# Taking the logarithm of the sums of squares straight out of PSUM, with the floor of the norm turned into a ceiling on its reciprocal

## The chip, the cores and the metric

The kernel runs on one core of one Trainium2 chip. The metric is the device time of one execution in microseconds (us), from the first to the last instruction of the core with what lies around it. A core has five engines that run side by side, each taking its own instructions in order: TensorE (PE, matrix multiplies; its weight loads are shown as PEld), VectorE (DVE), ScalarE (ACT), GpSimd (POOL) and SyncE (SP), which here only starts DMAs. They wait for each other through semaphores.

## The reference

The input is 8 sequences of 512 tokens with 128 features. A first block adds a causal attention with 16 heads. The second block, which the change concerns, is a stack of six layers. Each layer shifts half of the features by one token, projects to queries, keys and values of 16 heads of 64, divides each query and each key by its length, applies a rotary table, attends within windows of 32 tokens and projects back; then it runs a gated feed-forward part behind a layer normalisation:

```
def l2norm(t):
    return t / jnp.maximum(jnp.linalg.norm(t, axis=-1, keepdims=True), 1e-12)
...
q = l2norm(q) * qs
k = l2norm(k) * ksc
```

What is asked is the exact division by the norm, with a floor of 1e-12 on the norm.

## The kernel before

Stage 1 (the first block) is not touched. Stage 2 holds the residual of all tokens in SBUF and goes, in each of six layers, through 8 sequences, and each sequence in 8 steps: four groups of four heads (a quad) by two halves of 256 tokens. A step's work is a pipeline over several steps: the projection of a quad-half is made in step n, its sum of squares, logarithm and exponential in step n+1, the scaled queries and keys in n+2, scores and softmax in n+3, the weighted values in n+4 and the output projection in n+5 (LAG_MIX to LAG_WO are 1 to 5). The order of work on each engine is written out by hand in one function `step` per engine. After the 8 sequences a layer drains for six steps (s == NSEQ) and runs its feed-forward part; the next layer fills the pipeline anew.

The normalisation takes this way. ScalarE squares the projections (line 935, tile sq, 128x1024). GpSimd adds the two halves of each head (line 824). TensorE sums over the features of a head with a matrix of ones into one PSUM bank, ss_bank (line 1198). VectorE copies that bank to inv_norm in SBUF with a floor of 1e-24 (line 1064, called the guard below, semaphore guard_done). ScalarE takes the logarithm of it in place (line 950, Ln) and then exp(-0.5 x) (line 953, Exp). One step later VectorE multiplies the rotated queries and keys by it in one instruction (line 783, write_qk, tile qk).

The order within a step, around the change:

- TensorE: scores (lines 1167, 1177), transposes of the softmax (1157), sums of squares (1198), values (1209 to 1211), projections (1222 to 1224), weighted values (1246), output projection (1259). In step 5 of all sequences but the first it then makes the mean of the layer normalisation of the sequence before (ffn_mean, line 1130), and in step 6 the variance (ffn_var, line 1134). Both write ss_bank, which the sums of squares use too, so both wait until that bank has been read in this step: `pe.wait_ge(S["guard_done"], n)`.
- ScalarE: copy of the transposed softmax (891), four exponentials (901), copy of the values (924), in step 6 a square for the layer normalisation (868), four exponentials, Square (935), the copy of y out of PSUM (943), Ln (950), Exp (953).
- VectorE: row minima (1020), a copy of the transposed softmax (1047), write_qk (783), guard (1064), two reciprocals (1027), and the two products with the rotary tables (1082, 1087). In step 5 a residual add (1033) stands ahead, in step 6 the centring (991).
- GpSimd: the add of the squares (824), two adds for the rotation (802), in step 3 the rest of the tokens of the next sequence (815, tokens_rest), then two multiplications of the softmax by the inverse sums (811), each waiting for its reciprocal.

Of the kernel before, what the change touches and what calls it, by code (L numbers as in the profile page):

```python
# [21 lines left out]
ACT = mybir.ActivationFunctionType  # L22
ALU = mybir.AluOpType
# [563 lines left out]
LN_SCALE = 2.0 ** 16  # L587
NORM_FLOOR = 1e-24


def build_stage2(nc, d, res_sb, u_sb, out, depth):

    with ExitStack() as st:
        def sb(name, shape, dt=F32):
            return st.enter_context(nc.sbuf_tensor(name, shape, dt))

        def sem(name):
# [27 lines left out]
        eps = sb("s2_eps", [P, 1])  # L625
        ln_shift = sb("s2_ln_shift", [P, 1])

        xs_raw = sb("s2_xs_raw", [P, WIN + SEQ])
# [32 lines left out]
        names = ("const_in consts cast zeroed attn_w ffn_w tables w_high w_rest xs_in xs_high xs_rest proj_done sq_done sqadd_done prod_done "  # L661
                 "add_done ss_done guard_done log_done inv_done norm_done score_done max_done exp_done "
                 "rden_done probs_done tr_done pt_first pt_second v_mm v_done v_moved0 v_moved1 v_moved2 v_moved3 pv_done y_done wo_done attn_res "
# [18 lines left out]
        def live(s, p, lag, first):  # L682

            if first:
                return p >= lag
            return p < lag if s == NSEQ else True
# [4 lines left out]
        def place(p, lag):  # L691

            m = (p - lag) % STEPS
            return m // 2, m % 2, m % 2
# [83 lines left out]
        def write_qk(p):  # L778

            quad, toks, par = place(p, LAG_NORM)  # L780
            at = WIN + toks * TOKS
            by = inv_norm[:, par, :, :].unsqueeze(2).to_broadcast([P, 2, 2, TOKS])
            return nc.vector.tensor_tensor(qk[:, quad % 2, :, :, at:at + TOKS], rotated[:, par, :, :, :], by, ALU.mult)  # L783

        @block.gpsimd
        def _(pool):
# [6 lines left out]
            pool.memset(ln_shift[:, :], 0.5 * float(np.log(LN_SCALE))).then_inc(S["consts"], 1)  # L793
            pool.wait_ge(S["consts"], 4)

# [67 lines left out]
        def _(act):  # L863
            act.wait_ge(S["consts"], 4)

# [11 lines left out]
            def step(l, s, p, first):  # L877
# [52 lines left out]
                if full:  # L930

                    act.wait_ge(S["proj_done"], n + 1)
                    if not (first and p == 0):
                        act.wait_ge(S["ss_done"], n)
                    nc.scalar.activation(sq[:, :, :, :], proj_ps[:, :, :, :], ACT.Square)\  # L935
                      .then_inc(S["sq_done"], 1)
                if live(s, p, LAG_VALUE, first):
                    m = n - LAG_VALUE
                    act.wait_ge(S["pv_done"], m + 1)

                    if not (first and p < LAG_VALUE + 2):
                        act.wait_ge(S["wo_done"], m - 1)
                    nc.scalar.activation(y[:, place(p, LAG_VALUE)[2], :, :],
                                         vy_bank[:, :].rearrange("p (a t) -> p a t", a=2), ACT.Copy)\
                      .then_inc(S["y_done"], 1)
                if live(s, p, LAG_MIX, first):

                    m, par = n - LAG_MIX, place(p, LAG_MIX)[2]
                    act.wait_ge(S["guard_done"], m + 1)
                    nc.scalar.activation(inv_norm[:, par, :, :], inv_norm[:, par, :, :], ACT.Ln, scale=LN_SCALE)\  # L950
                      .then_inc(S["log_done"], 1)
                    act.wait_ge(S["log_done"], m + 1)
                    nc.scalar.activation(inv_norm[:, par, :, :], inv_norm[:, par, :, :], ACT.Exp, scale=-0.5,
                                         bias=ln_shift[:, 0:1]).then_inc(S["inv_done"], 1)
# [25 lines left out]
        def _(dve):  # L980
# [4 lines left out]
              .then_inc(S["cast"], 1)  # L985
            dve.wait_ge(S["consts"], 4)
            dve.wait_ge(S["cast"], 2)
# [23 lines left out]
            def step(l, s, p, first):  # L1011
# [38 lines left out]
                if norm:  # L1050
# [6 lines left out]
                    write_qk(p).then_inc(S["norm_done"], 1)  # L1057
                if live(s, p, LAG_MIX, first):
                    m, par = n - LAG_MIX, place(p, LAG_MIX)[2]
                    dve.wait_ge(S["ss_done"], m + 1)  # L1060

                    if not (first and p < LAG_MIX + 2):
                        dve.wait_ge(S["norm_done"], m - 1)
                    nc.vector.tensor_scalar(inv_norm[:, par, :, :].rearrange("p a t -> p (a t)"), ss_bank[:, :],
                                            NORM_FLOOR, None, ALU.max).then_inc(S["guard_done"], 1)
                if score:
# [56 lines left out]
        def _(pe):  # L1123
            pe.wait_ge(S["const_in"], 48)
            pe.wait_ge(S["consts"], 4)
            pe.wait_ge(S["cast"], 2)
# [17 lines left out]
            def step(l, s, p, first):  # L1144
# [41 lines left out]
                if live(s, p, LAG_MIX, first):  # L1186
# [3 lines left out]
                    if not (first and p == LAG_MIX):  # L1190
                        pe.wait_ge(S["guard_done"], m)

# [83 lines left out]
                if full and not first and p in (LN_STEP, LN_STEP + 1):  # L1276

                    pe.wait_ge(S["guard_done"], n)
                    (ffn_mean if p == LN_STEP else ffn_var)(l * NSEQ + s - 1)
# [142 lines left out]
```

## Time and profile before

| | us |
|---|---|
| runs shown: median (lowest to highest) | 4187.51 (4180.85 to 4187.87) |
| the profiled execution's own time | 4182.92 |
| its span, first to last instruction | 4181.1 |
| PE busy | 3900.5 (93%) |
| DVE busy | 3305.5 (79%) |
| ACT busy | 3091.6 (74%) |
| POOL busy | 2581.2 (62%) |

Stage 1 fills about the first 700 us; the six layers are alike after that, some 577 us each. The mean granted TensorE clock is 0.986 of full speed. "Busy" counts the time in which an engine has an instruction under way, and that includes time in which the instruction itself is held up inside the engine. Matmuls overlap, so their recorded durations are longer than what each adds to the chain.

### The profile page before, as it was taken

The numbers are of one execution on the slowest core, as the hardware profiler recorded it, in microseconds if no ns is written. First come the engines' busy times: TensorE is split into PE (matmuls) and PEld (weight loads), VectorE is DVE, ScalarE is ACT, GpSimd is POOL, SyncE is SP. The second block draws the span as 40 slices with busy tenths as digits, with TensorE's granted clock in tenths as the row PEclk, the third lists the DMA queues.
The fourth block names the chain that finished last, engine by engine and source line by source line (L and its number), as shares of the span: only waits on it lengthen the run. The fifth ranks groups of instructions, "written<-read, shape, count | busy, mean of one in ns | idle before, by whom it ended". The sixth has DMA issues, their size and how long they took to land.

```text
span 4181.1 us, 190344 instructions
## 1 busy us (share of the span) xinstructions
PE 3900.5 (93%) x78816; PEld 3039.7 (73%) x78816; DVE 3305.5 (79%) x5294; ACT 3091.6 (74%) x10376; POOL 2581.2 (62%) x2583
## 2 busy tenths in 40 slices
PE   6888885999998999989999989999899999899998
PEld 3555554888866888848888668888488887588884
DVE  6778874988866888938888668989489886698894
ACT  5877785888865888838888658888488886588883
POOL 4667765766645676627666456766377664566660
PEclk9999998999999999999999999999999999999999
DMA  1000001111111111111111111111111111111110
GB/s 35 2 2 2 2 2 53 47 45 45 46 56 38 45 47 45 44 50 44 49 44 46 58 36 47 44 49 42 53 44 47 47 44 61 35 45 46 47 43 26
DMA packets 100195, 167.40 MB, mean 40 GB/s; under 512 B 26224, under 2 KB 33648, under 8 KB 99056
## 3 DMA queue, kind: packets, MB, share of 16 engines
q1 hardware_dynamic: 99312, 154.89, 12.6%
q8 instruction: 644, 10.55, 1.1%
q14 instruction: 239, 1.96, 0.2%
HBM read 26.13 MB, written 2.10 MB: 7 GB/s over the span
## 4 chain that ended last, share of the span: by engine, by line
PE 69%; issue 9%; POOL 3%; DVE 1%; ACT 0%; DMA 0%; SPq 0%; POOLq 0%; DVEq 0%; ACTq 0%
PE s_bank L1177 13%; PE s_bank L1246 10%; PE s_bank L1259 9%; PE s_bank L1198 8%; PE s_bank L1157 5%; PE s_proj L1222 4%; PE s_proj L1223 4%; PE s_proj L1224 4%; PE s_bank L1209 2%; PE s_bank L1210 2%; PE s_bank L1211 2%; PE s_bank L1167 2%; PE s_bank L1140 1%; POOL s_rotated L802 1%; PE s_bank L1289 1%
## 5 line engine op out<-in xcount | busy, mean ns | idle before, releaser
L802 POOL TENSOR_TENSOR s_rotated<-s_rotated,s_by_sin 128x512 f32<-128x512 f32 x768 | 983.8, 1302 | 227.3 <-DVE s_by_sin L1087 225.2
L811 POOL TENSOR_TENSOR s_probs<-s_probs,s_rden 128x256 f32<-128x256 f32 x768 | 479.7, 641 | 729.8 <-DVE s_rden L1027 729.3
L901 ACT ACTIVATE s_probs<-s_bank,s_neg_max 128x64 f32<-128x64 f32 x3072 | 908.0, 310 | 5.7 <-DVE s_neg_max L1020 5.6
L783 DVE TENSOR_TENSOR s_qk<-s_rotated,s_inv_norm 128x1024 f32<-128x1024 f32 x384 | 743.8, 1937 | 11.5
L1082 DVE TENSOR_TENSOR s_rotated<-s_proj,s_cos 128x1024 f32<-128x1024 f32 x384 | 469.6, 1223 | 241.5 <-ACT s_sq L935 240.9
L901 ACT ACTIVATION_READ_ACCUMULATOR s_probs<-s_bank,s_neg_max 128x1 f32 x3072 | 636.1, 207 | 0.0
L891 ACT ACTIVATE s_probs_t<-s_bank 64x512 f32<-64x512 f32 x384 | 226.8, 591 | 524.8 <-PE s_bank L1157 524.8
L1177 PE MATMUL s_bank<-s_qk 32*32 32x64 f32 x49152 | 581.4, 223 | 26.3 <-issue 25.9
L1177 PEld LDWEIGHTS s_bank<-s_qk 32*32 32x32 f32 x49152 | 510.9, 103 | 115.4 <-issue 114.6
L213 POOL TENSOR_TENSOR s_probs<-s_probs,s_rden 128x384 f32<-128x384 f32 (+3 forms) x512 | 406.4, 802 | 206.1 <-DVE s_rden L406 202.2
L824 POOL TENSOR_TENSOR s_sq<-s_sq 128x512 f32<-128x512 f32 x384 | 490.2, 1277 | 65.5 <-ACT s_sq L935 59.8
L1087 DVE TENSOR_TENSOR s_by_sin<-s_proj,s_sin 128x1024 f32<-128x1024 f32 x384 | 466.2, 1214 | 0.0
L1246 PE MATMUL s_bank<-s_probs_t,s_v 128*64 128x64 f32 x12288 | 445.5, 226 | 21.8 <-ACT s_probs_t L891 17.1
L1246 PEld LDWEIGHTS s_bank<-s_probs_t,s_v 128*64 128x64 f32 x12288 | 393.0, 138 | 77.1 <-ACT s_probs_t L891 21.4
L1198 PE MATMUL s_bank<-s_sq,s_same_head 128*128 128x256 f32 x1536 | 403.9, 386 | 40.2 <-POOL s_sq L824 37.9
L1222 PE MATMUL s_proj<-s_xs_high,s_w_high 128*128 128x256 f32 x1536 | 437.1, 285 | 0.0
L1259 PE MATMUL s_bank<-s_y,s_wo 128*128 128x256 f32 x1536 | 436.9, 407 | 0.0
L1223 PE MATMUL s_proj<-s_xs_rest,s_w_high 128*128 128x256 f32 x1536 | 436.6, 284 | 0.0
L1224 PE MATMUL s_proj<-s_xs_high,s_w_rest 128*128 128x256 f32 x1536 | 435.2, 283 | 0.0
L935 ACT ACTIVATE s_sq<-s_proj 128x1024 f32<-128x1024 f32 x384 | 397.8, 1036 | 25.2 <-PE s_proj L1224 25.2
L1020 DVE TENSOR_REDUCE s_neg_max<-s_bank 128x4 f32<-128x256 f32 x768 | 289.0, 418 | 72.1 <-PE s_bank L1177 69.1
L295 ACT ACTIVATE s_probs<-s_bank,s_neg_max 128x384 f32<-128x384 f32 (+3 forms) x512 | 271.9, 533 | 89.3 <-DVE s_neg_max L397 85.7
(118 smaller groups left out, 8156.2 us busy)
## 6 DMA issues: line engine op xcount, KB each, us to landing
s_v<-s_v SPq DMA_DIRECT2D x384, 192.0 KB, 2.5
s_v<-s_v SPq DMA_DIRECT2D x384, 64.0 KB, 2.4
s_qk<-f_wqk SPq DMA_DIRECT2D x6, 1024.0 KB, 6.4
s_xs_raw<-u SPq DMA_DIRECT2D x48, 128.0 KB
s_xf<-u SPq DMA_DIRECT2D x48, 128.0 KB, 2.3
s_xs_raw<-u SPq DMA_DIRECT2D x48, 127.8 KB
s_xf<-u SPq DMA_DIRECT2D x48, 127.8 KB, 2.6
s_qk<-f_wv SPq DMA_DIRECT2D x6, 512.0 KB, 6.8
```

The costliest lines, as they stand in the source:

```text
L783: return nc.vector.tensor_tensor(qk[:, quad % 2, :, :, at:at + TOKS], rotated[:, par, :, :, :], by, ALU.mult)
L802: nc.gpsimd.tensor_tensor(rotated[:, par, :, half, :], rotated[:, par, :, half, :], by_sin[:, :, 1 - half, :], (ALU.subtract, ALU.add)[half])\
L811: nc.gpsimd.tensor_tensor(part, part, by, ALU.mult).then_inc(S["probs_done"], 1)
L824: nc.gpsimd.tensor_tensor(sq[:, :, 0, :], sq[:, :, 0, :], sq[:, :, 1, :], ALU.add)\
L901: last = nc.scalar.activation(probs[:, par, h, b, :], score_bank[h][:, b * KEYS:(b + 1) * KEYS], ACT.Exp, scale=-1.0, bias=neg_max[:, par, ...
L1177: last = nc.tensor.matmul(score_bank[e][to:to + WIN, w * KEYS:(w + 1) * KEYS], qk[rows, quad % 2, 0, c, WIN + at:WIN + at + WIN], qk[rows, ...
L1198: last = nc.tensor.matmul(ss_bank[:, i * TOKS:(i + 1) * TOKS], same_head[:, :], sq[:, i, 0, :], start=True, stop=True)
L1222: nc.tensor.matmul(proj_ps[:, i, c, :], w[0], xs_high[:, s % 2, at:at + TOKS], start=True, stop=False)
L1223: nc.tensor.matmul(proj_ps[:, i, c, :], w[0], xs_rest[:, s % 2, at:at + TOKS], start=False, stop=False)
L1224: last = nc.tensor.matmul(proj_ps[:, i, c, :], w[1], xs_high[:, s % 2, at:at + TOKS], start=False, stop=True)
L1246: last = nc.tensor.matmul(mixed[HD * h:HD * (h + 1), pair, t, :, e, :], v[:, cols, (half * NT + t) * 2 + e, at:at + HD], probs_t[:, e, t, ...
L1259: last = nc.tensor.matmul(wo_bank[:, half * TOKS:(half + 1) * TOKS], wo[:, 2 * quad + pair, :], y[:, par, pair, :], start=(p == LAG_WO and ...
```

## The change

VectorE's guard goes away. ScalarE's Ln now reads ss_bank in PSUM itself, with a small bias that takes the place of the floor, and moves ahead of the copy of y, right behind Square. The floor on the norm becomes a ceiling of 1e12 on its reciprocal, applied inside write_qk, which becomes two instructions of another kind (scalar_tensor_tensor, 128x512 each: minimum with a constant, then product) in place of one of 128x1024. Whatever waited for guard_done now waits for log_done: the next sums of squares on TensorE, and the mean and the variance of the layer normalisation, which share the bank. One small memset for the bias is added at the start.

```diff
@@ write_qk
-            by = inv_norm[:, par, :, :].unsqueeze(2).to_broadcast([P, 2, 2, TOKS])
-            return nc.vector.tensor_tensor(qk[:, quad % 2, :, :, at:at + TOKS], rotated[:, par, :, :, :], by, ALU.mult)
+            for i in range(2):
+                by = inv_norm[:, par, i, :].unsqueeze(1).to_broadcast([P, 2, TOKS])
+                last = nc.vector.scalar_tensor_tensor(qk[:, quad % 2, i, :, at:at + TOKS], by, NORM_CUT,
+                                                      rotated[:, par, i, :, :], ALU.min, ALU.mult)
+            return last
@@ ScalarE, step: between Square and the copy of y
+                if live(s, p, LAG_MIX, first):
+
+                    m, par = n - LAG_MIX, place(p, LAG_MIX)[2]
+                    act.wait_ge(S["ss_done"], m + 1)
+                    if not (first and p < LAG_MIX + 2):
+                        act.wait_ge(S["norm_done"], m - 1)
+                    nc.scalar.activation(inv_norm[:, par, :, :].rearrange("p a t -> p (a t)"), ss_bank[:, :], ACT.Ln,
+                                         scale=LN_SCALE, bias=log_floor[:, 0:1]).then_inc(S["log_done"], 1)
@@ ScalarE, step: behind the copy of y
-                    act.wait_ge(S["guard_done"], m + 1)
-                    nc.scalar.activation(inv_norm[:, par, :, :], inv_norm[:, par, :, :], ACT.Ln, scale=LN_SCALE)\
-                      .then_inc(S["log_done"], 1)
                     act.wait_ge(S["log_done"], m + 1)
@@ VectorE, step: behind write_qk
-                if live(s, p, LAG_MIX, first):
-                    m, par = n - LAG_MIX, place(p, LAG_MIX)[2]
-                    dve.wait_ge(S["ss_done"], m + 1)
-
-                    if not (first and p < LAG_MIX + 2):
-                        dve.wait_ge(S["norm_done"], m - 1)
-                    nc.vector.tensor_scalar(inv_norm[:, par, :, :].rearrange("p a t -> p (a t)"), ss_bank[:, :],
-                                            NORM_FLOOR, None, ALU.max).then_inc(S["guard_done"], 1)
@@ TensorE, step: ahead of the sums of squares, and ahead of the mean and the variance
-                        pe.wait_ge(S["guard_done"], m)
+                        pe.wait_ge(S["log_done"], m)
...
-                    pe.wait_ge(S["guard_done"], n)
+                    pe.wait_ge(S["log_done"], n)
                     (ffn_mean if p == LN_STEP else ffn_var)(l * NSEQ + s - 1)
```

## Rows read from the trace of the kernel before

**Rows 1.** Busy us by stretch: its length, PE, PEld, DVE, ACT, POOL, clock, DMA.

```profile
1386.50:1756.30 369.80, 365.25 (x9098) 312.82 (x9097) 329.41 (x457) 303.35 (x1080) 252.27 (x246) 1.00 0.16 46
```

**Rows 2.** Chain that ended last: start, us it adds, what; ends of steps 5 and 6.

```profile
1509.92 0.86 PE s_bank L1130 x2
...
1518.12 0.86 PE s_bank L1134 x2
```

**Rows 3.** Waits over the whole span: who for whom, us, times, longest.

```profile
POOL s_probs L811 <- DVE s_rden L1027: 729.3, 392, 6.6
ACT s_probs_t L891 <- PE s_bank L1157: 524.8, 384, 5.0
PE s_bank L1177 <- issue: 25.9, 41, 2.3
...
PE s_bank L1157 <- issue: 8.1, 12, 0.9
```

**Rows 4.** Timeline, step 5 of one sequence: start us, us, instruction, [idle before].

```profile
1507.17 0.69 DVE L1064 TENSOR_SCALAR s_inv_norm<-s_bank 128x512 f32<-128x512 f32 x1
...
1508.18 1.03 ACT L935 ACTIVATE s_sq<-s_proj 128x1024 f32<-128x1024 f32 x1
...
1509.08 0.61 ACT L943 ACTIVATE s_y<-s_bank 128x512 f32<-128x512 f32 x1
...
1509.76 1.02 PE L1130 MATMUL s_bank<-s_xf,s_mean_w 128*128 128x512 f32 x2
```

**Rows 5.** Timeline, step 6 of the same sequence.

```profile
1516.90 1.03 ACT L935 ACTIVATE s_sq<-s_proj 128x1024 f32<-128x1024 f32 x1
...
1517.80 0.61 ACT L943 ACTIVATE s_y<-s_bank 128x512 f32<-128x512 f32 x1
...
1517.95 1.02 PE L1134 MATMUL s_bank<-s_rstd,s_mean_w 128*128 128x512 f32 x2
```

**Rows 6.** Single lines: ns min/median/max, first and last start us.

```profile
L873 ACT ACTIVATE s_rstd<-s_bank,s_eps x48: 666/668/688, 819.5 to 4126.7; 128x512 f32<-128x512 f32 x48
...
L1134 PE MATMUL s_bank<-s_rstd,s_mean_w x96: 590/592/593, 817.8 to 4126.1; 128*128 128x512 f32 x96
```

**Rows 7.** Timeline in stage 1: a matmul that waits for ScalarE.

```profile
227.16 0.63 ACT L253 ACTIVATE s_sq<-s_xc 128x512 f32<-128x512 f32 x1
227.84 1.13 PE L451 MATMUL s_bank<-s_sq,s_mean_w 128*128 128x512 f32 x2 [0.47 <-ACT s_sq L253]
```

**Rows 8.** VectorE's groups: busy us, mean ns of one, idle before.

```profile
L783 DVE TENSOR_TENSOR s_qk<-s_rotated,s_inv_norm 128x1024 f32<-128x1024 f32 x384 | 743.8, 1937 | 11.5
L1082 DVE TENSOR_TENSOR s_rotated<-s_proj,s_cos 128x1024 f32<-128x1024 f32 x384 | 469.6, 1223 | 241.5 <-ACT s_sq L935 240.9
...
L1064 DVE TENSOR_SCALAR s_inv_norm<-s_bank 128x512 f32<-128x512 f32 x384 | 265.5, 691 | 14.2 <-PE s_bank L1198 2.8
...
L1092 DVE SCALAR_TENSOR_TENSOR u<-s_bank,s_vec,u 128x512 f32<-128x512 f32 x48 | 36.1, 751 | 63.0 <-PE s_bank L1289 63.0
```

**Rows 9.** Timeline of a step 3, and the sums of squares of step 4.

```profile
1366.51 2.52 POOL L802 TENSOR_TENSOR s_rotated<-s_rotated,s_by_sin 128x512 f32<-128x512 f32 x2 [0.44 <-DVE s_by_sin L1087]
...
1367.85 2.27 DVE L783 TENSOR_TENSOR s_qk<-s_rotated,s_inv_norm 128x1024 f32<-128x1024 f32 x1
...
1368.99 2.33 POOL L815 TENSOR_TENSOR s_xs_rest<-s_xs_raw,s_xs_high 128x544 fp32r<-128x544 f32 x1
...
1371.29 1.18 POOL L811 TENSOR_TENSOR s_probs<-s_probs,s_rden 128x256 f32<-128x256 f32 x2
...
1372.43 1.28 POOL L824 TENSOR_TENSOR s_sq<-s_sq 128x512 f32<-128x512 f32 x1
...
1374.01 0.73 PEld L1198 LDWEIGHTS s_bank<-s_sq,s_same_head 128*128 128x128 f32 x4
```

**Rows 10.** Timeline, step 3 while a layer's pipeline fills.

```profile
1888.63 1.87 DVE L783 TENSOR_TENSOR s_qk<-s_rotated,s_inv_norm 128x1024 f32<-128x1024 f32 x1
...
1891.52 0.38 PE L1167 MATMUL s_bank<-s_band_b,s_ident_b 128*128 128x256 bf16 x2 [1.20 <-ACT s_probs L901]
```

More of the change, by code:

```diff
@@ L587 @@
 LN_SCALE = 2.0 ** 16
-NORM_FLOOR = 1e-24
+NORM_CUT = 1e12
+LOG_FLOOR = LN_SCALE * 1e-32
 def build_stage2(nc, d, res_sb, u_sb, out, depth):
@@ L626, in build_stage2 @@
         ln_shift = sb("s2_ln_shift", [P, 1])
+        log_floor = sb("s2_log_floor", [P, 1])
         xs_raw = sb("s2_xs_raw", [P, WIN + SEQ])
@@ L661, in build_stage2 @@
         names = ("const_in consts cast zeroed attn_w ffn_w tables w_high w_rest xs_in xs_high xs_rest proj_done sq_done sqadd_done prod_done "
-                 "add_done ss_done guard_done log_done inv_done norm_done score_done max_done exp_done "
+                 "add_done ss_done log_done inv_done norm_done score_done max_done exp_done "
                  "rden_done probs_done tr_done pt_first pt_second v_mm v_done v_moved0 v_moved1 v_moved2 v_moved3 pv_done y_done wo_done attn_res "
@@ L793, in _ @@
             pool.memset(ln_shift[:, :], 0.5 * float(np.log(LN_SCALE))).then_inc(S["consts"], 1)
-            pool.wait_ge(S["consts"], 4)
+            pool.memset(log_floor[:, :], LOG_FLOOR).then_inc(S["consts"], 1)
+            pool.wait_ge(S["consts"], 5)
             def step(l, s, p, first):
@@ L863, in _ @@
         def _(act):
-            act.wait_ge(S["consts"], 4)
+            act.wait_ge(S["consts"], 5)
             def centred_square(f):
@@ L985, in _ @@
               .then_inc(S["cast"], 1)
-            dve.wait_ge(S["consts"], 4)
+            dve.wait_ge(S["consts"], 5)
             dve.wait_ge(S["cast"], 2)
@@ L1124, in _ @@
             pe.wait_ge(S["const_in"], 48)
-            pe.wait_ge(S["consts"], 4)
+            pe.wait_ge(S["consts"], 5)
             pe.wait_ge(S["cast"], 2)
```

## The prediction

> **What bounds the kernel now.** I read the busy time by stretch first. In 369.8 us that hold six whole sequences (48 steps, 7.70 us each) TensorE has work under way for 365.25 us, VectorE for 329.41, ScalarE for 303.35 and GpSimd for 252.27, at a granted clock of 1.00 [rows 1]. So TensorE is what sets the pace of a step, and an instruction taken off VectorE or moved on ScalarE buys nothing by itself. The chain of waits agrees: between the end of one step and the start of the next it names TensorE's own work one piece behind the other, the mean adding 0.86 us in step 5 and the variance 0.86 in step 6 [rows 2]. Then the waits: ScalarE waits 524.8 us in 384 steps for TensorE's transposes, 1.37 us a step, so every step of ScalarE starts anew from TensorE's transposes and what it does afterwards has a fixed distance to them; GpSimd waits 729.3 us for VectorE's reciprocals; and what TensorE loses for no reason that the profile shows is 25.9 us in the scores and 8.1 ahead of the transposes [rows 3]. So the question is only where the change makes TensorE wait for something that it does not wait for now.
>
> **Part 1: who frees the bank for the mean and the variance.** Both wait in their own step until ss_bank has been read. Now VectorE reads it: in the step shown the guard ends at 1507.17 + 0.69 = 1507.86, 1.9 us before the mean starts at 1509.76 [rows 4]. After the change the reader is ScalarE's Ln, which stands behind Square, and Square stands behind eight exponentials. The place that Ln gets is that of the copy of y today, which starts 0.13 us before Square's recorded end (1509.08 against 1508.18 + 1.03 = 1509.21) [rows 4]. A logarithm out of PSUM with a bias of the same shape takes 668 ns [rows 6]. So the bank comes free at 1509.08 + 0.67 = 1509.75. A matmul that waits for ScalarE starts 0.05 us after the release (227.16 + 0.63 = 227.79, start 227.84), and the pair then takes 1.13 us, where an unheld pair takes 1.02, because its weights could not be loaded ahead [rows 7, 4]. The mean would end at 1509.75 + 0.05 + 1.13 = 1510.93, against 1509.76 + 1.02 = 1510.78 now: 0.15 us later.
>
> In step 6 ScalarE has a square for the layer normalisation more ahead of Square, so it stands nearer to TensorE. Ln would run from 1517.80 to 1518.47, the variance start at 1518.52 and end at 1519.65, against 1517.95 + 1.02 = 1518.97 now [rows 5]: 0.68 us later. TensorE would stand idle from the end of the output projection.
>
> How often: the matmul of the variance has 96 records, two for each, so 48 in all [rows 6], of which one in each of six layers lies in the feed-forward part and waits for no bank. That leaves 42 of each kind. 42 x 0.15 = 6.3 us and 42 x 0.68 = 28.6 us, together 34.9 us. Nothing catches it up: TensorE is the pace, and ScalarE does not get ahead of it through the delay, since its next step starts from TensorE's transposes again [rows 3]. What comes behind (centring, the logarithm of the variance) shifts with TensorE. Bounds: if Ln cannot start before Square's recorded end, both waits are 0.13 longer, +11 us; if Ln is as quick as the copy of y (0.61 instead of 0.67), both are 0.06 shorter, -5 us.
>
> The other new wait, sums of squares for the Ln of the step before, costs nothing: they wait anyway for GpSimd's add, which starts after Square and takes 1.28 us [rows 9], while Ln ends 0.54 after Square.
>
> **Part 2: Ln on ScalarE.** Its length hardly changes, and it moves ahead of the copy of y. The copy becomes 0.54 us later; it is needed in the next step by the output projection, which ends each step of TensorE, and by the values some 4 us later. Exp ends where it did, since both orders hold the same three instructions. I take 0. What covers it is the 4 us of scores, transposes and sums on TensorE; without them the copy would cost 0.54 a step.
>
> **Part 3: VectorE.** The guard goes, 691 ns x 384 [rows 8]. write_qk becomes two instructions of a kind of which the trace shows only one with one operand in PSUM, at 751 ns for 128x512; today's takes 1937 on average where the same shape from PSUM takes 1223 [rows 8]. Two halves cost at least 2 x 0.75 - 1.22 = 0.28 us more than one, so VectorE gains 0.69 - 0.28 = 0.41 us a step, all of it idle time. From the other side: if the pair paid the full excess of today twice (1937 - 1223 = 714 ns more), it would be 0.3 us a step dearer, which still fits into 369.8 - 329.41 = 40.4 us of idle time in 48 steps, 0.84 a step [rows 1]. In both cases 0 for TensorE; I take the first.
>
> Where does today's excess come from? In a step 3 write_qk starts at 1367.85, GpSimd's two rotations end at 1366.51 + 2.52 = 1369.03, write_qk at 1370.12: 1.09 us after GpSimd was done. GpSimd's next instruction, tokens_rest, has begun at 1368.99 and ends when the softmax multiplication starts, at about 1371.3, 1.2 after write_qk [rows 9]. The two take turns, a whole instruction at a time. The Trainium skill states this (SBUF — State Buffer, "SBUF: two separate sides"): the pair of ports that VectorE and GpSimd share is an exclusive lock, and a VectorE instruction with two SBUF inputs holds it to its end. The trace agrees, with the 1.09 and the 1.2.
>
> For the split this means that in step 3 tokens_rest gets in between the halves. A half takes about 1.09 x 751/1223 = 0.67 once it is let in, or 0.62 if it saves the same 0.13 as the whole does; I take 0.62. Then: 1369.03 + 0.62 + 1.20 + 0.62 = 1371.47, the first reciprocal 0.2 later at 1371.67, where GpSimd starts on the softmax at 1371.29 now [rows 9]: 0.38 us later. Its add of the squares would end at 1372.43 + 1.28 + 0.38 = 1374.09, and the sums of squares start at 1374.01 now: 0.13 us of wait with the 0.05. The step shown is the tightest sort (0.30 between add and sums); I take half, 0.07, in 42 steps 3 us, with 0 and 0.38 x 42 = 16 as ends. In the other seven steps GpSimd has nothing to put between the halves, as it waits for VectorE's reciprocals there [rows 3].
>
> While a layer's pipeline fills, write_qk ends at 1890.50 and the scores of that quad start at 1891.52 [rows 10]. There both rotations compete with write_qk; with one (1.2 us) between the halves and the 0.28 it would end at about 1891.9, 0.4 later than the scores start. Six layers: 2 us, ends 0 and 6.
>
> **Sum.** 34.9 + 3 + 2 = 40 us on the profiled execution's 4182.9, that is 4223. The median shown is 4187.5, with the three runs from 4180.9 to 4187.9; against it the sum would be 4227.5. I forecast between the two, 4225.
>
> **The rivals.**
>
> A, not slower: TensorE's own halts absorb the new waits. The halts in the scores and ahead of the transposes, 25.9 + 8.1 = 34 us [rows 3], have no engine as releaser. If they are the instruction stream running dry, a TensorE that stands at a semaphore lets the stream get ahead, and the halts after it vanish. Price: 40 - 34 = 6 us, 4192. It decides from the point where a lead won in steps 5 and 6 lasts till the next halt. For it: the halts are few and of even size (25.9 / 41 = 0.63 us). Against it: most steps between two halts run without one, so what is fetched ahead seems bounded, and a lead in step 6 is used up long before. Chance 0.08.
>
> B, slower still: the two halves of write_qk let GpSimd in and the add of the squares becomes late. At the upper end of part 3, 16 + 6 in place of 3 + 2, with Ln as long as taken: 4185 + 35 + 22 = 4242. For it: the turns seen [rows 9]. Against it: there is slack of 0.3 us or more behind the add. By the rule of the Trainium skill named above, and with some GpSimd instruction between the halves in every step, the price would be far higher, some 1.2 us less the 0.41 gained and the 0.3 of slack; the waits for reciprocals speak against that [rows 3]. Chance 0.12.
>
> C, faster: VectorE, not TensorE, sets many steps. Each step that it sets would win 0.41 us, and from 40 / 0.41 = 98 of 384 steps on the change would pay; with half of the steps, 192 x 0.41 = 79 us less 40 gives 4146. For it: VectorE is under way 89% of the time and matmul records overlap, so TensorE's 99% flatters it [rows 1]. Against it: the chain has TensorE's own work at the ends of these steps [rows 2], and VectorE has 241.5 us of idle time before its first product alone [rows 8]. Chance 0.03.
>
> D, the change does less than it says: ScalarE lets Ln pass ahead so that the bank is free in time. It would need Square 0.7 us earlier. Nothing in the trace does that: 4187. Chance 0.04.
>
> **How the numbers follow.** Forecast 0.73, A 0.08, B 0.12, C 0.03, D 0.04. A measurement of this kernel can tell about 0.2% (8.4 us) from no change; so A and D are "same", C is "faster", the forecast and B are "slower": 0.85, with 0.03 for faster and 0.12 for same. The range: the forecast's own ends are 35 - 5 = 30 below and 35 + 11 + 5 = 51 above on a base of 4181 to 4187.5, 4211 to 4239; a part of A's giving back and B widen it to 4206 and 4246.
>
> **What would show it.** In the changed kernel the mean and the variance of steps 5 and 6 have ScalarE's Ln as releaser, with about 0.04 and 0.57 us of idle TensorE before them and the unloaded weights beside that; Ln starts right behind Square; a step 5 and a step 6 are 0.15 and 0.68 us longer, the other steps the same. VectorE's idle time grows by some 0.4 us a step. In step 3 the two halves have tokens_rest between them. I am wrong if the variance starts without a wait, if the steps other than 5 and 6 change by more than 0.05 us on average, or if the halts in the scores shrink by as much as the waits grow.

## The result and the profile after

The changed kernel takes 4223.28 us (median of six runs, 4218.89 to 4230.56); the kernel before takes 4184.5 us beside it (six runs, 4175.78 to 4187.87). The ratio is 1.0097, with a 95% interval of 1.0083 to 1.0111: slower by 39 us, where 40 were forecast (4225 us, measured 4223). The profiled execution took 4221.61 us, 38.7 more than the one before.

In the changed kernel the mean of the layer normalisation is line 1135, the variance 1139, the sums of squares 1203, Square 943, Ln 951, the copy of y 959, the transposes 1162, the scores 1182, the split product 788, tokens_rest 823, the add of the squares 832.

The busy time of six sequences, from one mean to the seventh after it, as in [rows 1] (columns: stretch, its length, PE, PEld, DVE, ACT, POOL, clock, DMA share, GB/s):

```profile
1393.70:1771.50 377.80, 370.16 (x9121) 312.68 (x9128) 304.34 (x458) 301.85 (x1081) 251.25 (x246) 1.00 0.16 45
```

VectorE works 25 us less in 48 steps, 0.52 us a step, and the stretch is 8.0 us longer. The timeline of steps 5 and 6 of the same sequence as in [rows 4, 5] shows where these are (start us, us, instruction, in brackets the engine's idle time before it and who ended it):

```profile
1516.84 1.03 ACT L943 ACTIVATE s_sq<-s_proj 128x1024 f32<-128x1024 f32 x1
...
1517.74 0.70 ACT L951 ACTIVATE s_inv_norm<-s_bank,s_log_floor 128x512 f32<-128x512 f32 x1
...
1518.57 1.12 PE L1135 MATMUL s_bank<-s_xf,s_mean_w 128*128 128x512 f32 x2
...
1525.81 1.03 ACT L943 ACTIVATE s_sq<-s_proj 128x1024 f32<-128x1024 f32 x1
...
1526.71 0.70 ACT L951 ACTIVATE s_inv_norm<-s_bank,s_log_floor 128x512 f32<-128x512 f32 x1
...
1527.46 1.13 PE L1139 MATMUL s_bank<-s_rstd,s_mean_w 128*128 128x512 f32 x2 [0.43 <-ACT s_inv_norm L951]
```

Ln starts 0.13 us before Square's recorded end and ends at 1526.71 + 0.70 = 1527.41; the variance starts 0.05 after it. TensorE is recorded idle for 0.43 us, and then the pair takes 1.13 us in place of 1.02; its weight load starts with it instead of ahead of it. The wait is longer than the recorded idle time, because matmul records overlap: in the kernel before the variance started at 1517.95, 0.16 us before the recorded end of the matmul ahead of it, and 0.43 + 0.16 = 0.59 us, where 0.57 were forecast. For the mean, which starts 0.15 us late, no idle time is recorded at all. The chain of waits, which had TensorE alone at this place [rows 2], now goes through ScalarE (start us, us that the piece adds, what):

```profile
1522.50 1.05 ACT s_probs L909 x7
...
1525.93 0.91 ACT s_sq L943
1526.84 0.58 ACT s_inv_norm L951
1527.46 1.13 PE s_bank L1139 x2
1528.59 0.22 PE s_bank L1172 x2
```

And over the whole span the waits, to be read against [rows 3] (who for whom, us in total, times, longest):

```profile
POOL s_probs L819 <- DVE s_rden L1040: 644.1, 518, 7.0
ACT s_probs_t L899 <- PE s_bank L1162: 600.4, 384, 5.4
...
PE s_bank L1182 <- issue: 30.1, 38, 2.4
...
PE s_bank L1139 <- ACT s_inv_norm L951: 18.0, 42, 0.4
```

The new wait of the variance is there 42 times. ScalarE waits 76 us more for the transposes. The halts in the scores (TensorE idle with no releaser in the profile) have not shrunk, they are 30.1 us where they were 25.9.

I also took the time from the sums of squares of one step to those of the next, for each place in a sequence, in every kernel of this study (medians over all sequences but the first of each layer, us). The mean and the variance come at the end of what is called step 5 and step 6 here. Steps 0 to 2 and 7 are the same everywhere to 0.03 (in step 0, where halts fall, to 0.1), so they are left out:

| kernel | step 3 | step 4 | step 5 | step 6 | ratio to before (95%) |
|---|---|---|---|---|---|
| before | 7.36 | 7.41 | 8.20 | 8.20 | 1 |
| changed | 7.34 | 7.63 | 8.45 | 8.90 | 1.0097 (1.0083 to 1.0111) |
| e1 Ln first in 5 and 6 | 7.35 | 7.62 | 8.29 | 8.27 | 1.0015 (1.0006 to 1.0023) |
| e2 Ln first in 6 | 7.34 | 7.62 | 8.45 | 8.20 | 1.0038 (1.0023 to 1.0053) |
| e3 one product | 7.35 | 7.64 | 8.46 | 8.90 | 1.0116 (1.0100 to 1.0132) |
| e4 split alone | 7.86 | 7.46 | 8.20 | 8.20 | 1.0035 (1.0021 to 1.0049) |
| e5 mean in another bank | 7.34 | 7.46 | 8.25 | 8.25 | 1.0016 (1.0006 to 1.0027) |
| e6 Ln behind y | 7.35 | 7.37 | 8.94 | 9.38 | 1.0213 (1.0198 to 1.0228) |
| e7 waits swapped | 7.35 | 7.49 | 8.45 | 8.90 | 1.0109 (1.0094 to 1.0124) |
| e8 Ln first everywhere | 7.75 | 7.47 | 8.63 | 8.27 | 1.0082 (1.0068 to 1.0097) |
| e9 centring between | 7.34 | 7.48 | 8.20 | 8.21 | 0.9995 (0.9986 to 1.0005) |

Step 4 has a halt in part of its instances, so its median jumps between 7.4 and 7.6 while its mean stays at 7.60 to 7.68 in all eleven traces.

### The profile page after: what moved, and what is told of

The parts are those of the page before. It is cut to its first block, busy times and chain, and to the rows that moved or that the text cites. A ratio compares the mean times of both kernels' runs of the same rounds, so it can differ in the third digit from the quotient of the medians.

```text
span 4219.7 us, 190345 instructions
## 1 busy us (share of the span) xinstructions
PE 3925.3 (93%) x78816; PEld 3035.9 (72%) x78816; DVE 3114.6 (74%) x5294; ACT 3074.2 (73%) x10376; POOL 2564.5 (61%) x2584
## 4 chain that ended last, share of the span: by engine, by line
PE 65%; issue 9%; ACT 5%; POOL 3%; DVE 0%; DMA 0%; SPq 0%; ACTq 0%; POOLq 0%; DVEq 0%
PE s_bank L1182 13%; PE s_bank L1251 9%; PE s_bank L1264 8%; PE s_bank L1203 7%; PE s_bank L1162 5%; PE s_proj L1229 4%; PE s_proj L1227 4%; PE s_proj L1228 4%; ACT s_probs L909 3%; PE s_bank L1172 2%; PE s_bank L1214 2%; PE s_bank L1215 2%; PE s_bank L1216 2%; PE s_bank L1145 1%; PE s_bank L1139 1%
## 5 line engine op out<-in xcount | busy, mean ns | idle before, releaser
L788 DVE SCALAR_TENSOR_TENSOR s_qk<-s_inv_norm,s_rotated 128x512 f32<-128x512 f32 x768 | 792.9, 1072 | 11.5
L1182 PE MATMUL s_bank<-s_qk 32*32 32x64 f32 x49152 | 583.5, 224 | 31.0 <-issue 30.1
```

Of the source, the lines that this page charges most:

```text
L788: last = nc.vector.scalar_tensor_tensor(qk[:, quad % 2, i, :, at:at + TOKS], by, NORM_CUT, rotated[:, par, i, :, :], ALU.min, ALU.mult)
L1182: last = nc.tensor.matmul(score_bank[e][to:to + WIN, w * KEYS:(w + 1) * KEYS], qk[rows, quad % 2, 0, c, WIN + at:WIN + at + WIN], qk[rows, ...
```

## The experiments

Theory W is that of the prediction: the whole loss is TensorE waiting, for the mean and the variance, for a Ln that stands behind Square.

**e1. Ln ahead of Square in steps 5 and 6.** All else as in the changed kernel; logarithm() holds the unchanged instructions of Ln.

```diff
+                log_first = ln and p in (LN_STEP, LN_STEP + 1)
+                if live(s, p, LAG_MIX, first) and log_first:
+                    logarithm()
                 if full:
 
                     act.wait_ge(S["proj_done"], n + 1)
...
-                if live(s, p, LAG_MIX, first):
+                if live(s, p, LAG_MIX, first) and not log_first:
+                    logarithm()
```

> The changed kernel, with one edit: in steps 5 and 6 of sequences 2 to 8, ScalarE takes Ln ahead of Square instead of behind it. Theory W (all of the loss is TensorE waiting, for the mean and the variance, for the Ln that stands behind Square): Ln ends 0.9 us earlier, in step 6 at about 0.6 us after the exponentials end, which is before TensorE wants the bank; both waits vanish and the time falls by 39 us to that of the kernel before, ratio 1.000 +- 0.001. Square comes 0.54 us later there, which the 2.3 us of slack between the add of the squares and the sums in steps 6 and 7 cover. Rival S (part of the loss is the split product and its turns with GpSimd): the split is still there, and with it its share, 5 us or more above the kernel before. Rival V (VectorE's relief is worth something that the waits hide): the time falls below the kernel before, ratio under 0.999.

Measured: 4185.98 us, ratio 1.0015 (1.0006 to 1.0023). Both waits are gone; the mean and the variance start where they did before. So 33 of the 39 us hang on the place of one instruction in 84 steps. But 6 us stay, which W did not foresee.

**e2. The same in step 6 only.**

```diff
-                log_first = ln and p in (LN_STEP, LN_STEP + 1)
+                log_first = ln and p == LN_STEP + 1
```

> As the run before it, but Ln goes ahead of Square in step 6 only. Theory W: only the wait of the variance goes, 42 x 0.69 = 29 us of the 39; what is left over the kernel before is the wait of the mean, 42 x 0.26 = 11 us, ratio 1.0026. If the two waits were not independent (the delay in step 5 shortening the one in step 6), the ratio would be nearer to 1.001 or to 1.005.

Measured: 4194.28 us, ratio 1.0038 (1.0023 to 1.0053), beside an expected 1.0026. Added up over all sequences but the first of a layer, step 6 is 0.5 us longer than before in its trace, where it was 29.0 longer in the changed kernel, and step 5 is 16.5 us longer, where it was 15.9. The two waits are independent. It also says that Ln ahead of Square costs nothing in step 6; the 6 us of e1 come from Ln's place in step 5.

The 16 us that are left are more than the 11 that were expected, and the median of step 5 (8.45) does not show why. In the sixth sequence of five layers, a halt of 1.1 to 1.4 us stands behind the mean, in the scores, six matmuls before their end. It stands there in every trace in which the mean waits for Ln (in e7 nine matmuls before the end): five times in the changed kernel and here, six times in e3, e6 and e7, 0.8 to 1.4 us each. In the kernel before, e1, e4, e5 and e9 the longest idle time in these scores is 0.5 us; e8, where the mean does not wait either, has two of 0.7. All halts in the scores and transposes behind the mean, over the 42 instances, are 5.3 to 6.7 us in the five traces and 0.2 to 2.5 in the six others. The changed kernel, this one, and the kernel before:

```profile
1066.48 0.31 PE L1182 MATMUL s_bank<-s_qk 32*32 32x64 f32 x6 [1.39 <-issue]
...
1062.18 0.31 PE L1187 MATMUL s_bank<-s_qk 32*32 32x64 f32 x6 [1.12 <-issue]
...
1059.47 1.48 PE L1177 MATMUL s_bank<-s_qk 32*32 32x64 f32 x128
```

So the wait for the mean costs 10.5 us by itself and some 5.5 more in halts that come with it. What causes them no run shows.

**e3. One product again, with no ceiling on the reciprocal.**

```diff
-            for i in range(2):
-                by = inv_norm[:, par, i, :].unsqueeze(1).to_broadcast([P, 2, TOKS])
-                last = nc.vector.scalar_tensor_tensor(qk[:, quad % 2, i, :, at:at + TOKS], by, NORM_CUT,
-                                                      rotated[:, par, i, :, :], ALU.min, ALU.mult)
-            return last
+            by = inv_norm[:, par, :, :].unsqueeze(2).to_broadcast([P, 2, 2, TOKS])
+            return nc.vector.tensor_tensor(qk[:, quad % 2, :, :, at:at + TOKS], rotated[:, par, :, :, :], by, ALU.mult)
```

> The changed kernel with VectorE's product undone: one instruction of 128x1024 again, without the ceiling on the reciprocal (that part of the computation is left out). Theory W: no change against the changed kernel, ratio to the kernel before 1.009 to 1.010; in step 3 the slack between the add of the squares and the sums grows again from 0.14 to 0.4 us or more, which nobody uses. Rival S: 5 us or more faster than the changed kernel, ratio 1.008 or less.

Measured: 4229.01 us, ratio 1.0116 (1.0100 to 1.0132). Nothing comes back; the ratio is above the expected 1.009 to 1.010, and the interval overlaps that of the changed kernel. The median slack between the add and the sums of step 4 grew from 0.14 to 0.36 us, and step 3 stayed at 7.35. The split has no share in the loss of the changed kernel: rival S falls.

**e4. The split alone, in the kernel before.** The diff of e3 the other way round, with the guard and Ln where they were.

> The kernel before, with the product alone split into the two new instructions; the guard stays on VectorE and Ln where it was. Theory W: TensorE waits for nothing new in steps 5 and 6. VectorE gets 0.28 us a step more work, which its idle time holds, but in step 3 tokens_rest gets between the halves (+1.2 us) and the guard is still behind them, so the add of the squares comes about 0.69 later than in the changed kernel, where 0.14 us of slack is left: a wait of some 0.5 us in 42 steps, 20 us, ratio 1.005, unless the reciprocals are not what that add waits for (then 1.000). Rival S expects a loss in every step, ratio above 1.008.

Measured: 4191.99 us, ratio 1.0035 (1.0021 to 1.0049), and the loss is in step 3 alone: 7.86 us in place of 7.36 in the median, added up 12.4 us. That is less than 42 x 0.50 = 21, since not every instance loses that much. In 32 of the 42 the sums start 0.05 us after the add; five others have 0.5 us of slack and take 7.32 us as before. And a halt and the wait behind it do not add up: the five instances with a halt of 0.3 us or more ahead of the sums take 7.77 to 8.22 us, where those with a wait and no halt reach 7.91. The timeline of step 3 and the start of step 4, as in [rows 9]:

```profile
1366.63 2.52 POOL L806 TENSOR_TENSOR s_rotated<-s_rotated,s_by_sin 128x512 f32<-128x512 f32 x2 [0.34 <-DVE s_by_sin L1091]
...
1367.98 3.50 DVE L785 SCALAR_TENSOR_TENSOR s_qk<-s_inv_norm,s_rotated 128x512 f32<-128x512 f32 x2
...
1369.11 1.81 POOL L819 TENSOR_TENSOR s_xs_rest<-s_xs_raw,s_xs_high 128x544 fp32r<-128x544 f32 x1
...
1371.50 0.69 DVE L1068 TENSOR_SCALAR s_inv_norm<-s_bank 128x512 f32<-128x512 f32 x1
...
1373.50 1.27 POOL L828 TENSOR_TENSOR s_sq<-s_sq 128x512 f32<-128x512 f32 x1
...
1374.82 0.73 PEld L1202 LDWEIGHTS s_bank<-s_sq,s_same_head 128*128 128x128 f32 x4 [0.65 <-POOL s_sq L828]
```

The two halves take 3.50 us where one product took 2.27, with tokens_rest (it ends at 1370.92) between them. Then the guard, the reciprocals, the softmax and the add of the squares are all late, and TensorE's sums of squares wait. So the split does cost 12 us in a kernel that keeps the guard; in the changed kernel it costs nothing, because there is no guard of 0.69 us behind it. The same place in the changed kernel:

```profile
1374.81 3.47 DVE L788 SCALAR_TENSOR_TENSOR s_qk<-s_inv_norm,s_rotated 128x512 f32<-128x512 f32 x2
...
1375.94 1.80 POOL L823 TENSOR_TENSOR s_xs_rest<-s_xs_raw,s_xs_high 128x544 fp32r<-128x544 f32 x1
...
1379.59 1.27 POOL L832 TENSOR_TENSOR s_sq<-s_sq 128x512 f32<-128x512 f32 x1
...
1380.98 0.73 PEld L1203 LDWEIGHTS s_bank<-s_sq,s_same_head 128*128 128x128 f32 x4
```

The add ends at 1380.86, 0.12 us before the sums start. Where they wait for the add, in e4, they start 0.05 us after its end; so here they do not wait, with 0.07 us to spare.

**e5. The mean and the variance of steps 5 and 6 in the bank of the transposes.**

```diff
@@ TensorE
-                    pe.wait_ge(S["log_done"], n)
-                    (ffn_mean if p == LN_STEP else ffn_var)(l * NSEQ + s - 1)
+                    (ffn_mean if p == LN_STEP else ffn_var)(l * NSEQ + s - 1, tr_bank)
@@ TensorE: ahead of the transposes instead of the sums of squares
+                    if full and not first and p == LN_STEP + 1:
+                        pe.wait_ge(S["f_xc"], l * NSEQ + s)
+                    if full and not first and p == LN_STEP + 2:
+                        pe.wait_ge(S["f_log"], l * NSEQ + s)
```

The centring and the logarithm of the variance read that bank too.

> The changed kernel, with the mean and the variance of steps 5 and 6 written to the bank of the transposes, which has been read by then, and so without any wait for Ln; the wait for their readers moves from the sums of squares to the transposes of the next step, 0.6 us earlier. Ln stays behind Square, the product stays split. Theory W: the loss goes, ratio 1.000 +- 0.001. A second theory, D, for the 6 us that stayed when Ln went ahead of Square (the later Square made VectorE's centring late, for which the sums of squares of step 6 wait): the centring is at its old time here, but the transposes want it 0.6 us earlier than the sums did, so up to 0.1 us in 42 steps may stay, 4 us. If the split product were what costs those 6 us, they would stay here in any case, spread over all steps.

Measured: 4187.69 us, ratio 1.0016 (1.0006 to 1.0027). Ln stays behind Square and the wait for the bank is gone by other means, and 32 of 39 us with it. So it is the shared bank, not the order on ScalarE as such. Steps 5 and 6 keep 0.05 us each, 4 us in all, about what was expected, but not for the reason that was expected. The transposes of the step behind start 0.19 us after the start of the last of the scores, where it is 0.14 in the kernel before, and this behind the mean as behind the variance. By then the centring has been done for 0.20 us and the logarithm of the variance for 0.42. So it is not these readers that are late. In e5 two instructions with waits stand ahead of the transposes, where one stands in the kernel before; that the second one is the 0.05 us is likely, but no run shows it alone. The rest of the 7 us is halts and spread.

**e6. Ln behind the copy of y,** still reading the bank itself: the block of Ln is moved behind the block of the copy.

> The changed kernel with Ln behind the copy of y, where it was before the change; it still reads the bank itself and still frees it. Theory W: Ln ends one copy (0.48 us from start to start) later in every step, so both waits grow by 0.48: 84 x 0.48 = 40 us more than the changed kernel, ratio to the kernel before 1.019. If TensorE's halts for instructions took part of the waits back, clearly less than 40. If the time hangs on how much ScalarE has to do rather than on where Ln stands, no change against the changed kernel.

Measured: 4267.92 us, ratio 1.0213 (1.0198 to 1.0228). That is 45 us over the changed kernel by the medians and 49 by the ratios, where 40 were expected. Both waits grow by the copy, and the mean now has one of its own in the list:

```profile
PE s_bank L1139 <- ACT s_inv_norm L960: 38.6, 42, 0.9
...
PE s_bank L1182 <- issue: 35.1, 46, 2.4
...
PE s_bank L1135 <- ACT s_inv_norm L960: 20.0, 42, 0.5
```

The waits for ScalarE are 38.6 + 20.0 = 58.6 us, 40.6 more than the 18.0 of the changed kernel. Steps 5 and 6 together are 44.0 us longer than in the changed kernel. The more TensorE waits for Ln, the more it loses, at least one for one, and nothing of these waits is given back: rival A falls for them.

**e7. The two waits ahead of the mean swapped.**

```diff
-                    pe.wait_ge(S["log_done"], n)
-                    (ffn_mean if p == LN_STEP else ffn_var)(l * NSEQ + s - 1)
+                    if p == LN_STEP:
+                        ffn_mean(l * NSEQ + s - 1, n)
+                    else:
+                        pe.wait_ge(S["log_done"], n)
+                        ffn_var(l * NSEQ + s - 1)
```

Inside ffn_mean the wait for log_done follows the one for xf_in.

> The changed kernel; TensorE ahead of the mean waits first for the tokens' DMA and then for Ln, instead of the other way round. In the trace of the changed kernel the mean starts 0.125 us after Ln's end and the variance, whose last wait is Ln's only where no other follows, 0.052. Theory O (a wait that is followed by another one is an instruction of its own and costs 0.07 us after the release): the mean starts 0.052 after Ln as well and step 5 is 0.07 us shorter, 3 us in all, in the trace; too small for the ratio (1.009). Otherwise the 0.125 stays.

Measured: 4227.93 us, ratio 1.0109 (1.0094 to 1.0124). The mean's weights start 0.113 us after Ln's end, in place of 0.124 (the variance: 0.051 in both), and step 5 stays at 8.45. But the run does not test theory O, for the swap in the source did not bring Ln's wait onto the weight load. In both traces the wait for Ln stands on an instruction of its own in TensorE's queue, and the weight load of the mean waits for the tokens' DMA; only the kind of that instruction changed (the changed kernel, then e7):

```profile
L1134 PEldq FUSED_REGOPS  x48: 37/37/42, 812.3 to 4149.8; - x48
...
L1136 PEldq EVENT_SEMAPHORE  x42: 51/51/51, 811.9 to 4107.8; - x42
```

For the variance, Ln's wait stands on the weight load itself. The other distances on record speak for theory O: sums that wait for the add, with that wait on their weight load, start 0.05 us after it (e4, e8), and sums that wait for the centring, with that wait on an instruction of its own, 0.115 us after it (36 of 42 in e1 and in e8). No run changed the place of a wait and nothing else, so theory O is neither shown nor refuted.

**e8. Ln ahead of Square in every step.**

```diff
-                log_first = ln and p in (LN_STEP, LN_STEP + 1)
+                log_first = True
```

> The changed kernel with Ln ahead of Square in every step. The waits in steps 5 and 6 go as they did where only these had Ln first, and the 6 us of the late centring stay. What is new: Square, VectorE's products, the rotations and write_qk are 0.54 us later in steps 0 to 4 and 7. Behind the add of the squares there is 1.2 us of slack in most steps, so nothing there; ahead of the sums of step 4, 0.14 only, because tokens_rest stands between the halves in step 3: a wait of 0.4 us in 42 steps, 17 us. Ratio 1.0055. If the slack of the other steps were not real, every step would lose, ratio above 1.01.

Measured: 4214.03 us, ratio 1.0082 (1.0068 to 1.0097); expected 1.0055. The wait came where it was expected, ahead of the sums of step 4: 0.4 us in the median, but 9.4 us added up over before instead of 17, since again not every instance waits. In the waits it shows as 40 cases, 16 more than the 24 of the changed kernel. Beside it the sums of squares of step 6 wait for the centring (s_xc); that I had priced as in e1, and it is longer here:

```profile
PE s_bank L1208 <- POOL s_sq L832: 40.4, 40, 2.5
...
PE s_bank L1208 <- DVE s_xc L1009: 6.8, 23, 0.4
```

Step 5 is 8.63 us, 0.34 longer than in e1, and added up 15.1 us longer than before, where it was 4.8 in e1: 10 us more than the expectation had, against 8 less in step 3. Of the 30 us that this trace is longer than the one before, 5.7 are from layer to layer, also not expected. The other steps lose nothing: their slack, about 1.2 us or more between the add and the sums in the median of the changed kernel, is real.

**e9. e1 with the centring between the two products of step 5.** After e1 there was a second theory, D: Ln ahead of Square in step 5 makes Square 0.54 us later, with it VectorE's products, and so the centring that stands behind them at the start of step 6. For its reading of ss_bank the sums of squares of step 6 wait. The trace of e1:

```profile
1513.62 1.21 DVE L1097 TENSOR_TENSOR s_by_sin<-s_proj,s_sin 128x1024 f32<-128x1024 f32 x1
...
1514.75 0.68 DVE L1009 TENSOR_TENSOR s_xc<-s_xf,s_bank 128x512 f32<-128x512 f32 x1
...
1515.55 0.73 PEld L1208 LDWEIGHTS s_bank<-s_sq,s_same_head 128*128 128x128 f32 x4
```

The centring ends at 1515.43 and the sums start 0.12 us later, the same distance that the mean has to Ln. In 36 of the 42 instances of e1 it is 0.115 us, where the kernel before has 0.53 in the median.

```diff
-                if ln and p == LN_STEP + 1:
-                    centre(l * NSEQ + s - 1)
...
+                    if ln and p == LN_STEP:
+                        centre(l * NSEQ + s - 1)
                     if not (first and p == 0):
                         dve.wait_ge(S["add_done"], 2 * n)
```

> The kernel with Ln ahead of Square in steps 5 and 6, and one edit more: VectorE centres the tokens for the layer normalisation between the two products of step 5 instead of at the start of step 6. Theory D (the 6 us that stayed there are TensorE's sums of squares of step 6 waiting for a centring that the later Square made late): the centring ends some 1.2 us earlier, well before the sums, steps 5 and 6 are back at 8.19 us from 8.28, and the ratio at 1.000 +- 0.001. If those 6 us belong to the split product or to something in all steps, the ratio stays at 1.0015.

Measured: 4178.86 us against 4181.74, ratio 0.9995 (0.9986 to 1.0005). Steps 5 and 6 are at 8.20 and 8.21 us. The centring ends 1.10 us ahead of the sums:

```profile
1514.53 1.23 DVE L1090 TENSOR_TENSOR s_rotated<-s_proj,s_cos 128x1024 f32<-128x1024 f32 x1 [1.30 <-ACT s_sq L954]
...
1515.67 0.68 DVE L1009 TENSOR_TENSOR s_xc<-s_xf,s_bank 128x512 f32<-128x512 f32 x1
...
1517.45 0.73 PEld L1208 LDWEIGHTS s_bank<-s_sq,s_same_head 128*128 128x128 f32 x4
```

Theory D of the experiments holds. With two edits of order the change costs nothing (within the interval, 6 us less to 2 us more), and VectorE has 3192.7 us of work where it had 3305.5. It does not beat the kernel before, and no run pointed to a version that would.

## Why the prediction was right

**What bounds the kernel.** Right. VectorE lost 191 us of busy time over the kernel (3305.5 to 3114.6) and TensorE took no notice; e9, with both waits removed and the centring early, ends where the kernel before does, so rival C had no more in it than the interval of e9 leaves, 6 us.

**The variance.** Forecast 0.68 us in each of 42 steps, measured 0.70: 42 x 0.70 = 29.4 us, 29.0 by the trace's own sum over step 6. e2 takes just this away.

**The mean.** The wait is where it was forecast, but this is the term that was mis-sized. Forecast 0.15, measured 0.25 (8.20 to 8.45). Two small parts were short: Ln out of PSUM takes 702 ns and not 668 (+0.03, L951 below), and the mean starts 0.124 us after Ln and not 0.05 (+0.07). That is 42 x 0.25 = 10.5 us where 6.3 were forecast. For the variance the longer Ln counts too: 0.68 + 0.03 = 0.71, measured 0.70. Step 5 as a whole gained 15.9 us, since in five of 42 instances it is 1.1 to 1.7 us longer by a halt. These halts are no accident of one trace: they stand at the same place in all five traces in which the mean waits for Ln (e2), and there step 5 adds up to 16 to 17 us over before in the four where the wait is of this length. So the wait for the mean cost 16 us and not 6; the forecast had nothing for the halts.

```profile
L951 ACT ACTIVATE s_inv_norm<-s_bank,s_log_floor x384: 681/702/748, 724.7 to 4122.2; 128x512 f32<-128x512 f32 x192
...
L788 DVE SCALAR_TENSOR_TENSOR s_qk<-s_inv_norm,s_rotated x768: 675/693/1842, 727.1 to 4128.2; 128x512 f32<-128x512 f32 x192
```

(columns as in [rows 6]: times, then ns min/median/max).

**The split product.** A half takes 693 ns where nothing is in its way; I had 751, from the one row of the kind that the trace had [rows 8]. So VectorE gained 0.5 us a step and not 0.41. In step 3 the turns came as worked out: write_qk as a whole took 3.47 us, forecast 1371.47 - 1367.85 = 3.62. The 3 us that I charged for it did not come: the add of the squares ended 0.12 us before the sums started, where I had it end 0.08 after their old start. The halves are quicker than I had them, which gives 0.15 of these 0.20 us. e4 shows that the mechanism is worth 12 us as soon as the guard stays behind it.

**The filling of the pipeline.** The wait in each layer's first scores is now for write_qk, as forecast, and it is 8.3 / 6 = 1.38 us long, 0.18 more than the 1.20 of [rows 10]; 1 us in all, forecast 2 (the forecast's own terms give 1890.50 + 1.20 + 0.28 = 1891.98 and not 1891.9, so 3):

```profile
PE s_bank L1172 <- DVE s_qk L788: 8.3, 6, 1.4
```

**The sum.** By the trace: steps 5 and 6 +45.0 us, the other steps of the later sequences -0.5, the first sequence of each layer with the filling -5.8, from layer to layer -3.2, stage 1 and the ends +3.1: 38.6. The minus 9 of the filling and the layers' ends were not foreseen. Part of it is the halts ahead of each layer's first values, which went from 10.8 to 7.4 us; why, the runs do not say. It need not belong to the change: the first sequences of the six layers take 349.0 us here, the lowest of the eleven traces, whose others have 351.6 to 356.2. So the mechanism was right, but that 40 meets 39 so closely is luck: steps 5 and 6 lost 10 us more than their 34.9, nearly all of it with the mean, and against it stand the 3 us of the split that did not come and the 9 us less at the layers' ends.

**The rivals.** A (halts give the waits back): not for the waits of steps 5 and 6. The halts in the scores are 25.9, 30.1 and 35.1 us from before to the changed kernel to e6, and in the same step they came with the mean's wait. The total says little by itself, since it is 15.1 to 29.4 us in the kernels whose mean does not wait. For a wait ahead of the sums something of A is true: in e4 a halt took the place of the wait behind it, and the halts of step 4 were 4.9 and 4.5 us in e4 and e8, where the other traces have 7.8 to 10.4. B: e3 shows no share of the split. C is dealt with above. D of the prediction (Ln in time by itself) did not occur; e1 shows that it takes an edit.

## What to carry to other kernels

When the reader of a shared buffer is moved to another engine, look at every instruction that waits for the buffer, not only at the next in the data's own path: here two matmuls of a layer normalisation, behind the same semaphore in 84 of 384 steps, paid the loss, and nothing on the way of the norms themselves was late. Work out the release from the new reader's place in its engine's queue; a wait that needs an instruction 0.7 us sooner is cheaper to mend by order than by speed. And try the mend on its neighbours: putting Ln first made another reader of the same bank late, and that took a second edit to see.

## What the runs showed of the hardware

- VectorE's product and GpSimd's instructions, all with their operands in SBUF, take turns by whole instructions. Split in two, the product lets a waiting GpSimd instruction in between: 3.50 us for the pair in e4, where one product took 2.27 [rows 9]. The Trainium skill (SBUF — State Buffer, "SBUF: two separate sides") states the turns: the shared pair of ports is an exclusive lock that is held for the whole instruction. The traces agree: 2.27 us for the whole product [rows 9], and in the split one GpSimd's tokens_rest between the halves (3.50 us in e4, 3.47 in the changed kernel).
- The half with the broadcast operand and two operators takes 693 ns for 128x512, less than the 751 of the same kind with an operand in PSUM [rows 8].
- A weight load that waits for ScalarE started 0.050 to 0.053 us after the release in the variance and 0.123 to 0.130 in the mean, in each of the 42 cases, whether the wait was short or long (e6). In the mean Ln's wait stands on an instruction of its own ahead of the weight load, in the variance on the weight load; in e7, with another kind of instruction for it, the mean has 0.113. Whether the place of the wait is the cause is open.
- TensorE's halts without a releaser stood in the scores in every trace, 15.1 us in all in e4 and 35.1 in e6. Where the mean waited for Ln, a halt of 0.8 to 1.4 us stood in the scores behind it in the sixth sequence of five or six of the six layers (five traces); where it did not, the longest there was 0.7 (six traces).
